# The down projection's rest of 42 rows in two passes, with the low parts stacked under the high ones

## What is computed

```python
h = (h - mu) / jnp.sqrt(var + 1e-05) * lg + lb
h = h @ w1 + b1
a, g = jnp.split(h, 2, axis=-1)
h = a * jax.nn.gelu(g, approximate=False)     # HID = 682 hidden features
x = x + h @ w2 + b2                           # the down projection
```

## Time and profile before

| | us |
|---|---|
| median of 3 runs | 2047.69 |
| lowest and highest | 2045.26, 2047.88 |
| the profiled execution | 2045.3 |
| its span, first to last instruction | 2043.5 |
| TensorE busy in it | 1900.0 (93%) |
| ScalarE busy | 1386.6 (68%) |
| VectorE busy | 1327.4 (65%) |
| GpSimd busy | 960.7 (47%) |
| mean granted clock of TensorE, share of full | 0.989 |

### The profile page before, as it was taken

One profiled execution on the slowest core, in us unless ns is written; L12 is line 12 of the kernel. 1 busy time (PEld: TensorE's weight loads), 2 busy tenths in 40 slices (PEclk: granted clock), 3 DMA queues, 4 the chain that ended last, 5 costly groups with the idle time before them and its releaser, 6 DMA issues.

```text
span 2043.5 us, 42506 instructions
## 1 busy us (share of the span) xinstructions
PE 1900.0 (93%) x15184; PEld 1576.0 (77%) x15184; DVE 1327.4 (65%) x4125; ACT 1386.6 (68%) x3869; POOL 960.7 (47%) x1311
## 2 busy tenths in 40 slices
PE   6999999999999789999999999999999999999998
PEld 4778777777777668778788787787887878878777
DVE  4544543444443467777768777787777776877775
ACT  5886877778678465775766757657567575675764
POOL 2432442434243463644726537457265473663732
PEclk9999999999999889999999999999999999999999
DMA  3322231313225411010110101304101011010010
GB/s 127 109 80 66 75 118 44 97 60 88 92 66 162 151 39 32 19 43 12 45 45 12 42 22 37 104 6 161 55 6 52 22 45 55 22 42 27 31 33 27
DMA packets 122261, 121.10 MB, mean 59 GB/s; under 512 B 27188, under 2 KB 100804, under 8 KB 122052
## 3 DMA queue, kind: packets, MB, share of 16 engines
q1 hardware_dynamic: 118884, 112.10, 17.2%
q10 hardware_dynamic: 3168, 6.29, 0.9%
HBM read 72.72 MB, written 37.25 MB: 54 GB/s over the span
## 4 chain that ended last, share of the span: by engine, by line
PE 32%; DVE 20%; ACT 9%; issue 3%; POOL 3%; DVEq 0%; ACTq 0%; SPq 0%; POOLq 0%
PE f_bank L1383 11%; PE f_scores L1523 5%; PE f_scores L1461 4%; ACT f_prob L1598 4%; DVE f_u L1751 4%; PE f_bank L1509 4%; PE f_bank L1469 4%; DVE f_gu L1748 2%; PE f_o_bank L1484 2%; ACT f_u L1618 2%; PE f_bank L1434 2%; DVE y_tok L1734 2%; DVE y_tok L1740 1%; POOL f_prob L1336 1%; DVE f_rstd L1727 1%
## 5 line engine op out<-in xcount | busy, mean ns | idle before, releaser
L1336 POOL TENSOR_SCALAR f_prob<-f_prob,f_row_inv 128x256 f32<-128x256 f32 x512 | 263.0, 532 | 331.2 <-DVE f_row_inv L1694 331.1
L587 POOL TENSOR_SCALAR a_prob<-a_prob,a_row_inv,a_gate 128x128 f32<-128x128 f32 x512 | 224.4, 455 | 407.8 <-DVE a_row_inv L927 407.8
L1383 PE MATMUL f_bank<-weights,f_actT 128*128 128x512 f32 x1152 | 301.8, 406 | 1.6 <-DVE f_actT L1637 1.6
L1509 PE MATMUL f_bank<-f_hT,f_w 128*128 128x256 f32 x2112 | 276.2, 286 | 7.6 <-DVE f_gu L1748 7.6
L1509 PEld LDWEIGHTS f_bank<-f_hT,f_w 128*128 128x128 f32 x2112 | 261.9, 190 | 14.2 <-DVE f_gu L1748 10.7
L1598 ACT ACTIVATE f_prob<-f_scores,f_neg_max 128x256 f32<-128x256 f32 x512 | 235.8, 487 | 32.6 <-DVE f_neg_max L1686 31.6
L1383 PEld LDWEIGHTS f_bank<-weights,f_actT 128*128 128x128 f32 x1152 | 208.4, 191 | 50.3 <-ACT f_probT L1545 5.4
L1686 DVE CUSTOM_DVE_ANT_0 f_scores<-f_scores,f_mask 128x256 f32<-128x256 f32 x512 | 199.8, 456 | 14.8 <-PE f_scores L1461 14.7
L1312 POOL TENSOR_TENSOR f_norm<-f_norm,f_minus_half 128x16 f32<-128x16 f32 x64 | 198.6, 3104 | 21.5 <-DVE f_norm L1646 18.9
L1618 ACT ACTIVATE f_u<-f_gu 128x256 fp32r<-128x256 f32 x192 | 80.2, 418 | 179.4 <-DVE f_gu L1748 179.4
L819 ACT ACTIVATE a_prob<-a_scores,a_neg_max 128x128 f32<-128x128 f32 x512 | 179.5, 390 | 27.8 <-DVE a_neg_max L918 26.5
(11 more groups left out here) (129 smaller groups left out, 3834.5 us busy)
## 6 DMA issues: line engine op xcount, KB each, us to landing
split_weights<-a_hi_lo SPq DMA_DIRECT2D x16, 512.0 KB, 2.8
x_next<-states SPq DMA_DIRECT2D x32, 256.0 KB, 3.2
tables<-scaled_tables SPq DMA_DIRECT2D x16, 512.0 KB, 6.2
f_x<-states SPq DMA_DIRECT2D x16, 512.0 KB, 5.5
split_weights<-a_hi_lo SPq DMA_DIRECT2D x12, 682.0 KB, 4.2
weights<-split_weights ACTq DMA_DIRECT2D x6, 1024.0 KB, 9.7
f_w<-split_weights SPq DMA_DIRECT2D x4, 1280.0 KB, 10.8
a_x_tok<-in_x SPq DMA_DIRECT2D x8, 512.0 KB, 4.4
```

The lines of the kernel that those rows point to most:

```text
L587: last = nc.gpsimd.tensor_scalar(part, part, row_inv[:, a % 2, head, t:t + 1], gate[:, half, t, h:h + 1], ALU.mult, ALU.mult)
L1336: last = nc.gpsimd.tensor_scalar(part, part, row_inv[:, a % 2, head, t:t + 1], 1.0, ALU.mult, ALU.mult)
L1383: last = nc.tensor.matmul(out, lhs(c, a), rhs(c, b), start=(i == 0), stop=(i == len(order) - 1))
L1509: mm = nc.tensor.matmul(out[:, which * PART:(which + 1) * PART], w1[:, wp, c, col:col + P], hT[:, hp, c, columns_of(a // FH)], start=(i == ...
```

## The change

For the short tile (j = 5) VectorE writes the low part no longer into the LO half of `u` but into the HI half, on the partitions 64 to 105 (`STACKED`), under the high part on 0 to 41. The high part of the short tile's weights is loaded a second time, to the same partitions 64 to 105 of `w2`, by one more transfer in each layer. One pass over the partitions 0 to 105 then computes high x high and low x high together, and a second, over 42 rows, high x low. For each tile of 128 tokens these two passes come one after the other. The partitions between, 42 to 63, hold zero weights; GpSimd sets that tile of `w2` and the odd slots' HI half of `u` to zero at the start of the phase, and the first layer's `load_others` waits for that. TensorE waits for four transfers of `w2` in place of three.

```diff
--- before.py
+++ after.py
@@ -994,6 +994,7 @@
         NU = HALVES * UNITS
         PARTS = 2
         PART = CHUNK // PARTS
+        STACKED = slice(P // 2, P // 2 + HL)
 
         wqkv = layer_projections(kept.weights)
         wo = kept.weights[:, 2 * CT * 3 * F_INNER:KEPT_WEIGHTS].rearrange("p (t c n) -> p t c n", t=2, c=PAIRS)
@@ -1223,6 +1224,7 @@
                 for part in (HI, LO):
                     sp.dma_start(w2[:, part, 0:FH - 1, :].bitcast(F32), weights[part, 0:full, :].rearrange("(j p) n -> p j n", p=HT)).then_inc(w2_loaded, 16)
                 sp.dma_start(w2[0:HL, :, FH - 1, :].bitcast(F32), weights[:, full:HID, :].rearrange("t p n -> p t n")).then_inc(w2_loaded, 16)
+                sp.dma_start(w2[STACKED, HI, FH - 1, :].bitcast(F32), weights[HI, full:HID, :]).then_inc(w2_loaded, 16)
 
             sp.wait_ge(kept.rows_loaded, 16 * FIRST_ROWS)
             sp.sem_inc(x_loaded.sem, 32)
@@ -1231,6 +1233,7 @@
             sp.wait_ge(filled.sem, filled.past(None, ("transpose_x", HALVES - 1), CT - 1))
             load_rows(0, HALVES - 1)
             sp.wait_ge(pad_zeroed, 1)
+            sp.wait_ge(zeroed, 1)
             load_others(0)
             sp.wait_ge(zeroed, 1)
             sp.wait_ge(kept.attended_stored, attended_end)
@@ -1300,7 +1303,9 @@
             pool.memset(minus_half[:], -0.5)
             pool.memset(edge[:], 0.0)
             pool.memset(w1[:, :, :, REST:REST + P].bitcast(F32), 0.0).then_inc(pad_zeroed, 1)
-            pool.memset(kT[:, :, 0:P], 0.0).then_inc(zeroed, 1)
+            pool.memset(kT[:, :, 0:P], 0.0)
+            pool.memset(w2[:, HI, FH - 1, :].bitcast(F32), 0.0)
+            pool.memset(u[:, 1::2, HI, :].bitcast(F32), 0.0).then_inc(zeroed, 1)
             pool.wait_ge(zeroed, 1)
 
             pool.sem_inc(x1_biased.sem, 1)
@@ -1513,16 +1518,17 @@
                     elif kind == "down":
                         j, m = hidden_of(a)
                         if a == 0:
-                            pe.wait_ge(w2_loaded, loads(3, layer))
+                            pe.wait_ge(w2_loaded, loads(4, layer))
                         pe.wait_ge(u_ready.sem, u_ready.past(it, ("up", a)))
                         if j == 0:
 
                             pe.wait_ge(exped.sem, exped.past(it, ("scores", (a // (PARTS * FH) + 1) * UNITS - 1), 1))
+                        order = [(m, up, wp) for up, wp in PASSES] if j < FH - 1 else [(STACKED.stop, HI, HI), (m, HI, LO)]
                         for t in (0, 1):
-                            for i, (up, wp) in enumerate(PASSES):
-                                mm = nc.tensor.matmul(y_banks[a // FH % PARTS][:, t, :], u[0:m, a % (2 * TILES), up, t * P:(t + 1) * P],
-                                                      w2[0:m, wp, j, :], start=(j == 0 and t == 0 and i == 0),
-                                                      stop=(j == FH - 1 and t == 1 and i == 2), skip_group_check=True)
+                            for i, (k, up, wp) in enumerate(order):
+                                mm = nc.tensor.matmul(y_banks[a // FH % PARTS][:, t, :], u[0:k, a % (2 * TILES), up, t * P:(t + 1) * P],
+                                                      w2[0:k, wp, j, :], start=(j == 0 and t == 0 and i == 0),
+                                                      stop=(j == FH - 1 and t == 1 and i == len(order) - 1), skip_group_check=True)
                         mm.then_inc(downed.sem, 1)
 
             for it in range(0, BATCH - 1):
@@ -1748,8 +1754,9 @@
                         nc.vector.scalar_tensor_tensor(out=gu[0:m, a % 2, :], in0=bank[n % 3][0:m, place:place + PART], scalar=b1_cols[0:m, 0, j:j + 1],
                                                        in1=gu[0:m, a % 2, :], op0=ALU.add, op1=ALU.mult).then_inc(emptied.sem, 1)
                         dve.wait_ge(u_hi.sem, u_hi.past(it, (kind, a)))
-                        nc.vector.tensor_tensor(u[0:m, a % (2 * TILES), LO, :], gu[0:m, a % 2, :],
-                                                u[0:m, a % (2 * TILES), HI, :].bitcast(F32), ALU.subtract).then_inc(u_ready.sem, 1)
+                        place = u[0:m, a % (2 * TILES), LO, :] if j < FH - 1 else u[STACKED, a % (2 * TILES), HI, :]
+                        nc.vector.tensor_tensor(place, gu[0:m, a % 2, :], u[0:m, a % (2 * TILES), HI, :].bitcast(F32),
+                                                ALU.subtract).then_inc(u_ready.sem, 1)
                     elif kind == "out":
                         dve.wait_ge(downed.sem, downed.past(it, ("down", (a + 1) * FH - 1)))
                         dve.wait_ge(attended_added.sem, attended_added.past(it, ("add_attended", a // PARTS)))
```

## The result

The changed kernel took 2050.22 us in the median of 17 runs, the kernel before 2044.76 in 17 runs beside them. The ratio is 1.0024 with a 95% interval of 1.0016 to 1.0033: 4.9 us slower (3.3 to 6.7); the two medians themselves are 5.5 us apart.

The account below looks back on a forecast made before the run. TensorE's own queue was taken to bound the stretch with the short steps. 12.6 us of added borders less 7.6 us of saved passes gave 5.0 us on the 2047.7 median: 2052.7 us, range 2046.5 to 2057.

Parts of the forecast that it names:

- The size and its sign: TensorE's short steps: 7.6 us saved by fewer passes, 12.6 us added by full-to-short borders, 5.0 us slower in sum.
- VectorE's low part: VectorE writing the low part from partition 64 on: cost zero, at most 0.3 us in all, and covered.
- The price of a border in a run of one: Drain between a 106-row and a single 42-row pass: taken as 0.197 us, between nothing and 0.20.
- Rival (a): Short steps: a single 42-row pass between wide ones causes no drain, so 7.6 us come back, 2040.1 us; chance 0.07.
- One for one to the end: All 32 short steps: what TensorE's queue gains or loses there reaches the kernel's end in full, 0.31 us a half-sequence.
- Rival (b): Borders partly hidden, or delay taken up by a later VectorE or ScalarE wait: sum zero, 2047.7 us; chance 0.16.
- The covers: GpSimd memsets (at most 1.3 us) and SyncE's new transfer issue (0.9 to 1.1 us) fall in idle time: cost zero.
- Rival (c): TensorE's clock falls in two more stretches because of more pauses, 3.4 us on top of 5.0: 2056.1 us; chance 0.03.

Follow-up runs that it names:

- wide_then_short: Changed kernel with both 106-row passes of a short step first, then both 42-row ones (106, 106, 42, 42); 5.5 us less than the kernel before.
- all_wide: Changed kernel with the second pass of a short step also over 106 rows, low weights of rows 42 to 105 zero; 6.1 us less than the kernel before.
- three_passes_wide: Kernel before with the three passes of a short step over all 128 rows, still six passes, added weight rows zero; 0.6 us less than the kernel before.
- setup_only: Changed kernel with its six 42-row passes and the low part's old place restored, memsets and tenth transfer kept; 0.2 us less than the kernel before.
- second_64_rows: Changed kernel with the second pass over 64 rows in place of 42 (106, 64, 106, 64), added weights zero; 4.7 us slower than the kernel before.
- all_wide_down6_first: Changed kernel with both passes over 106 rows and `down 6` moved ahead of `up 10`; 10.8 us less than the kernel before, median 2033.38 us.

## Why the prediction was right, point by point

**The size and its sign.** 64 passes at 0.119 us less and 64 borders at 0.197 us more gave +5.0; +4.9 was measured. Each factor was then measured apart. Borders alone gave +13.1 against 12.6. Passes alone, in wide_then_short, gave -5.5 against -7.6. The pieces agree to 0.01 us: 1.06 us for `down 5` against the 1.07 forecast, and 0.14 us more for `down 11` against 0.15. The mechanism is thus right, but that the total agrees to 0.1 us is in part luck. In the profiled execution a cost that the sum had at zero, VectorE's 0.1 us in each half-sequence (see VectorE's low part, below), and a wait elsewhere that was missing in three of them, 0.45 us each, nearly cancel.

**The price of a border in a run of one.** This had no row, and the measured border was taken for it, against a lower bound of nothing. The loads 0.31 us apart inside the step, against 0.12 in a run, put it at 0.19 us. Rival (a), the passes alone, would have needed loads at 0.12.

**One for one to the end.** This held in the direction that was forecast, in the mean of 15 half-sequences (0.30 us each against 0.29 in the two steps) though not in each of them, and in that direction only. The step of the prediction said "what TensorE's queue gains or loses in them"; all_wide shows that it does not hold for gains: VectorE's work on the banks stands about 0.2 us behind `down 5` there. In three_passes_wide, whose gain is smaller, 0.36 of 0.41 us a half-sequence came as long as the clock was full. Of the 0.87 us that all_wide was to save in a half-sequence, 0.24 lie in `down 11` and came (2.98 us with the scores against 3.24); 0.63 lie in `down 5`, and of these 0.16 came. The chain of before could not show it, since a chain names the last wait and not the one that comes next. Rival (b), a later wait that takes up a delay, was put down for the losing direction. In 12 of the 15 half-sequences nothing took the delay up; the wait that is missing in the other three lies 35 us behind it, and whether the delay moved it no run shows.

**The covers.** GpSimd's two memsets took 0.30 and 0.94 us, 1.2 in place of the 1.3 bounded, and it then idled for 7.14 us. The new transfer's issue took 0.59 and 0.39 us, below the 0.9 to 1.1 that half of the 84 KB transfer gave; the next issues came at 730.13 and 1416.44, 28 and 7 us behind its end, so the cover held:

```profile
683.43 0.30 POOL L1307 MEMSET f_w<- 128x256 f32 x1
683.68 0.94 POOL L1308 MEMSET f_u<- 128x1024 f32 x1
691.77 6.05 POOL L1317 TENSOR_TENSOR f_norm<-f_norm,f_minus_half 128x16 f32<-128x16 f32 x2 [7.14 <-DVE f_norm L1652]
...
701.74 0.59 SPq L1227 DMA_DIRECT2D f_w<-split_weights  x1
730.13 0.38 SPq L1204 DMA_DIRECT2D x_next<-states  x1
...
1408.88 0.39 SPq L1227 DMA_DIRECT2D f_w<-split_weights  x1
1416.44 0.68 SPq L1259 DMA_DIRECT2D f_kT<-f_kT  x1
```

**VectorE's low part.** The prediction put its cost at zero, at most 0.3 us in all, from the length of the operation. That length is indeed the 0.42 us that it was on its own partitions. What it costs is behind it. The operation that follows it began 0.07 to 0.08 us ahead of its end and now begins 0.03 us behind it (once 0.08), at all 32 places; in setup_only, with the low part in its old place, it is ahead again. Before, and after:

```profile
2038.06 0.68 DVE L1757 TENSOR_TENSOR f_x<-f_scores,f_x 128x512 f32<-128x512 f32 x1
...
2042.04 0.42 DVE L1758 TENSOR_TENSOR f_u<-f_gu,f_u 42x256 fp32r<-42x256 f32 x1 [0.48 <-ACT f_u L1624]
...
2042.49 0.69 DVE L1764 TENSOR_TENSOR f_x<-f_scores,f_x 128x512 f32<-128x512 f32 x1
```

In the first part of each half-sequence that next operation is the multiplication that empties the bank for `up 9`, which TensorE waits for. This is why its 15 waits are 12.6 us in place of 10.7, 1.9 us more, in the change and in second_64_rows alike, and 12.5 in all_wide_down6_first. Whether the other partitions or the other half of `u` bring the 0.1 us no run separates.

**The clock.** Rival (c) needed further stretches at 1.2 GHz, worth 3.4 us. Over the 15 half-sequences both profiled executions have the same slowed stretches, the tail of one in the first 3 us and one near 1461 us before and 1463 us after, so the 4.5 us more are found at an equal clock. The mean of the 17 runs is 0.9881, at most 0.0011 below what the kernel before had in any session, so by 1 to 2 us per 0.001 up to some 2 us of the 4.9 may be the clock's; most of it is not.

## What to carry to other kernels

Count a product's passes together with the changes between passes of up to 64 rows and wider ones: here such a change cost 0.2 us, as much as 1.7 passes of 256 columns, so passes of one kind belong together, or the short ones padded with zero weights to 65 rows or more (both done, with `down 6` moved ahead of `up 10`, the kernel took 2033.38 us, 0.53% below the kernel before, 0.40 to 0.66). A chain of waits tells what a delay costs but not what a gain brings: before counting on a gain, look for the wait that stands just behind the shortened work, here for the bank that VectorE empties. And compare the granted clock before comparing times: 0.002 of it hid some 3 us of what four kernels had gained.

## What the runs showed of the hardware that was not expected

Wide passes over zeros are no dearer than short ones: six passes over 128 rows, of which 86 hold zero weights, advance the chain by 0.71 us, as six full ones do. The border is as sharp as one row: 2047.71 us with 64 rows in the second pass, 2039.99 with 65, though each streams the same 256 columns and the added row adds nothing to the sum. An operation of VectorE that writes its 42 rows from partition 64 on, into the other half of the tile, takes no longer itself, but the next one begins 0.1 us later (0.03 us behind its end in place of 0.07 ahead of it, 32 of 32). And the granted clock fell in four half-sequences in a row of one profiled execution (0.76 over 14 us), though in the 5 us ahead of the fall TensorE had the same 28 matmuls as in the kernel before, where it stayed at 1.00; what decides this the runs do not show.
